# Splitting and turning the maxima of attention 2 one operation at a time, among the next stage's units

## Chip, cores and metric

One core of a Trainium2 chip. The metric is the device time of one execution in microseconds (us). Three runs of the kernel before give 2128.75, 2121.38 and 2128.39 us, so the median is 2128.39.

## What is computed

Two pre-norm blocks over x of shape (4, 512, 256): attention and a mixture of 12 experts, then a second attention and a mixture of 8 experts. The change lies in the second attention, whose keys and values are given:

```python
def _L1_attn_ref(query, kv_k, kv_v, Wq, Wo):     # query = layernorm(x), 4 x 512 rows
    HEADS = 16; HEAD_DIM = 16; SCALE = 1.0 / np.sqrt(HEAD_DIM)
    Q = (query @ Wq.T).reshape(B, QL, HEADS, HEAD_DIM)
    K = kv_k.reshape(KV, HEADS, HEAD_DIM)        # KV = 32 * 128 = 4096 keys
    V = kv_v.reshape(KV, HEADS, HEAD_DIM)
    scores = jnp.einsum('bqhd,khd->bhqk', Q, K) * SCALE
    attn = jax.nn.softmax(scores, axis=-1)
    out = jnp.einsum('bhqk,khd->bqhd', attn, V).reshape(B, QL, HIDDEN)
    return out @ Wo.T
```

## The kernel before, in words

**Stages.** Attention 2 runs in 32 stages (STAGES). A stage H is one pair of heads with the 512 queries of one of the 4 batches: for 4 groups of 4 heads (g), for 4 batches (i), for 2 pairs (h). Within a stage the 4096 keys are taken in 16 steps (NM, the index m; G = 16 H + m counts them over all stages). A step has 4 score products (scores, L1678: 128 keys by 512 queries of one head each, two keys tiles by two heads), 4 exponentials on ScalarE (L1813), and 2 halves of the value products of the step before (values, L1693). Scores are written to three PSUM banks in turn, and the product of a bank waits for the exponential that last read it.

**Maxima.** The softmax subtracts each query's maximum, and it does so inside the score product: two extra rows of the query operand hold the negative maximum, split into a high and a low part, against rows of ones in the keys. So the maxima of stage H + 1 must be known before its first score. They are found while stage H runs, in 32 units (NH). A unit is two products of 128 queries by 512 keys (max_unit, L1096) into one of two pairs of banks, and one reduction over them on VectorE (max_reduce, L1102). TensorE may start a unit when VectorE has done with the unit two before it (the semaphore unit_taken).

**The end of a set of maxima.** After its last unit VectorE makes four small operations, each waiting for the one before:
- max_total (L1112): the maximum over the parts, negated, 128 x 8;
- max_high (L1116): its high part, rounded to the type of the products;
- max_low (L1120): the rest, as a second such number;
- max_turned (L1126): a transpose that puts the parts in rows; it tells rows_ready.

SP then writes the rows to DRAM (store_maxima, L1078), waits for that, reads them into the extra rows of the query operand (load_maxima, two DMAs of L1085) and waits for their landing (L1632). TensorE waits for the same landing (rows_in, L1772) before the first score of the stage.

**The order of the work** is written out by schedule() (L1503). The units of stage H + 1 lie in the steps from G = 16 H - 4 (0 for H = 0) to 16 (H + 1) - 5, two in each step; in TensorE's program one stands after the first two scores of a step and one after the last two. So a set of maxima is complete 4 steps (AHEAD) before its stage begins, and the next step holds the first two units of the set after it. The plan also holds a few other units: late queries (steps 1, 3, 6 and 9 of stages 1 and 3) and, in the last two stages, the output products of earlier batches with residual and normalization (front_results, L1872; steps 11, 12, 14, 15, 16 and so on, counted from the first step of stage 30). The last set of maxima, of stage 31, ends in step 11, where the first front unit stands too, and no maxima follow it. The function unit of VectorE's program (L1824) does what VectorE has to do for one entry of the plan; the loop at L1897 calls it for each step's entries.

**Other queues.** SP also does, in each stage, the fold of the value sums (L1545, L1551), the reciprocals' way through DRAM (L1557, L1560), the packing of outputs (L1569), the loads of keys, values and queries of the next group of heads, and at stage 24 those of the last block's weights. VectorE's reciprocal of the sums (L1870) stands alone between two units, in step 6. GpSimd (POOL) adds and scales the sums (L1650, L1655).

Of the kernel before, what the change touches and what calls it, by code (L numbers as in the profile page):

```python
# [52 lines left out]
def build(nc, a, out):  # L53
    with ExitStack() as ctx:
# [75 lines left out]
        def f32(t):  # L130

            return t.bitcast(F32)
# [860 lines left out]
        with ExitStack() as l1:  # L993
# [110 lines left out]
            def new_maxima(H):  # L1104
                h = H % NP
                return mneg[:, 2 * TB * h:2 * TB * (h + 1)].rearrange("p (r t) -> p r t", r=2)

            def new_parts(H, s):
                return mparts[:, :, s, TB * (H % NP):TB * (H % NP + 1)]
# [4 lines left out]
            def max_high(dve, H):  # L1114
                dve.wait_ge(max_done, H + 1)
                nc.vector.tensor_copy(new_parts(H, 0), new_maxima(H)).then_inc(high_done, 1)  # L1116

            def max_low(dve, H):
                dve.wait_ge(high_done, H + 1)
                nc.vector.tensor_tensor(new_parts(H, 1), new_maxima(H), f32(new_parts(H, 0)), ALU.subtract).then_inc(low_done, 1)  # L1120

            def max_turned(dve, H):
                dve.wait_ge(low_done, H + 1)
                if H:
                    dve.wait_ge(rows_out, 16 * H)
                nc.vector.transpose(mrows[:], f32(mparts[:]).rearrange("p r s n -> p (r s n)")).then_inc(rows_ready, 1)  # L1126
# [376 lines left out]
            def schedule():  # L1503

                plan = [[] for _ in range(STAGES * NM)]
                for H in range(STAGES - 1):
                    begin, end = H * NM - (AHEAD if H else 0), (H + 1) * NM - AHEAD
                    done = 0 if H else EARLY
                    for u in range(done, NH):
                        plan[begin + (u - done) * (end - begin) // (NH - done)].append(("max", H + 1, u))  # L1510
                for c, H in LATE.items():
                    for n, m in enumerate(LATE_AT):
                        plan[H * NM + m].append(("late", c, n))
                for b, kts in enumerate(FRONTS):
                    for n, kt in enumerate(kts):
                        plan[(BATCHES - 1) * NKT + kt].append(("front", b, n))
                return plan

            EARLY = 6
            plan = schedule()  # L1520
# [14 lines left out]
            def unit_bank(n):  # L1535
                return 3 + 2 * (n % 2) if n < LAST_UNIT else WIDE
# [44 lines left out]
            with nc.Block() as block:  # L1581
# [237 lines left out]
                @block.vector  # L1819
                def _(dve):  # L1820
                    ch = Chain(dve, steps[0])
                    units = 0

                    def unit(kind, i, u):  # L1824
                        nonlocal units
                        base = unit_bank(units)
                        dve.wait_ge(unit_mm, units + 1)
                        if kind == "max":
                            max_reduce(NP * u + i % NP, i, base).then_inc(unit_taken, 1)
                            if u == NH - 1:  # L1830
                                wait_unit(dve, units)
                                max_total(i).then_inc(max_done, 1)
                                max_high(dve, i)
                                max_low(dve, i)
                                max_turned(dve, i)
                        elif kind == "late":
                            late_results(i, u, base)
                        elif kind == "front":
                            front_results(i, u, base)
                        elif kind == "turn_out":  # L1840
                            view = ps[:, base, 0:TB * 2 * VR].rearrange("p (t h c) -> p t h c", t=TB, h=2)
                            ch(nc.vector.reciprocal(orec[:], view[:, :, :, DH]))
                            ch.wait()
                            dst = outT[:].rearrange("p (t q h d) -> p t q h d", t=TB, q=2, h=HG)[:, :, (NG - 1) % 2, HG - 2:HG]
                            for t in range(TB):
                                w = nc.vector.tensor_tensor(dst[:, t], view[:, t, :, 0:DH],
                                                            orec[:, t, :].unsqueeze(2).to_broadcast([P, 2, DH]), ALU.mult)
                            w.then_inc(unit_taken, 1)
                        else:
                            rows = slice((NG - 1) % 2 * HG * DH + 2 * DH, (NG - 1) % 2 * HG * DH + HG * DH)  # L1850
                            nc.vector.tensor_copy(aT[rows, NB - 1, (NG - 1) // 2, :], ps[rows, base, :]).then_inc(unit_taken, 1)
                        units += 1

                    def late_results(c, n, bank):
                        m = n % KD
                        if n < KD:
                            nc.vector.tensor_copy(xnT[:, m, :], ps[:, bank, :]).then_inc(unit_taken, 1)
                        else:
                            if c == 3 and m == 0:
                                dve.wait_ge(q_stored, 16 * KD * 3)  # L1860
                            nc.vector.tensor_copy(late_q[:, 0, m], ps[:, bank, :]).then_inc(q_split, 1)
                            dve.wait_ge(q_split, KD * c + m + 1)
                            nc.vector.tensor_tensor(late_q[:, 1, m], ps[:, bank, :], f32(late_q[:, 0, m]), ALU.subtract
                                                    ).then_inc(q_left, 1)
                            dve.wait_ge(q_left, KD * c + m + 1)
                            nc.vector.engine_nop().then_inc(unit_taken, 1)

                    def reciprocals(H):
                        dve.wait_ge(sums_in, 16 * 2 * (H + 1))
                        nc.vector.reciprocal(sums[:], sums[:]).then_inc(rec_done, 1)  # L1870

                    def front_results(b, n, bank):  # L1872
                        rows = lambda t: x[:, TB * b + t, :]
                        if n in (2, 3):
                            nc.vector.tensor_copy(xT1[b][:, n % 2, :], ps[:, bank, :]).then_inc(unit_taken, 1)
                        elif n in (0, 1):
                            t = TB * b + 2 * n
                            nc.vector.tensor_tensor(x[:, t:t + 2, :].rearrange("p t d -> p (t d)"),
                                                    x[:, t:t + 2, :].rearrange("p t d -> p (t d)"), ps[:, bank, :],
                                                    ALU.add).then_inc(unit_taken, 1)  # L1880
                            if n == 1:
                                wait_unit(dve, units)
                                norm_stats(dve, NB + b, rows, main)
                                dve.wait_ge(main.rstd_done, NB + b + 1)
                                if b:
                                    dve.wait_ge(rows1_out, 16 * b)
                                for t in range(TB):
                                    nc.vector.tensor_scalar(xn[:, t, :], rows(t), main.meanvar[:, t, 0:1], main.rstd[:, t:t + 1],
                                                            ALU.subtract, ALU.mult).then_inc(main.norm_done, 1)
                        else:  # L1890
                            take_logits(ch, bank, b, unit_taken)

                    RECIPROCAL = 6

                    for e in first:
                        unit(*e)
                    for G in range(STAGES * NM):  # L1897
                        H, m = divmod(G, NM)
                        if H and m == RECIPROCAL:
                            reciprocals(H - 1)  # L1900
                            if H == STAGES - 1:
                                nc.vector.tensor_tensor(fold, ident[:, 0:2 * VR], ident[:, 2 * VR:4 * VR], ALU.add).then_inc(fold_made, 1)
                        for e in plan[G]:
                            unit(*e)
                    for e in tail:
                        unit(*e)
            clear(step, *main.norm_sems, *l1_used)
# [536 lines left out]
```

## Time and profile before

| what | value |
|---|---|
| median of three runs | 2128.39 us |
| the profiled execution | 2126.7 us |
| its span, first to last instruction | 2125.0 us |
| mean granted TensorE clock | 0.947 |
| PE busy | 1972.1 us, 93% of the span |
| VectorE (DVE) busy | 1559.6 us, 73% |
| ScalarE (ACT) busy | 1346.0 us, 63% |
| GpSimd (POOL) busy | 334.3 us, 16% |

The span is cut into instructions of each engine; PE is TensorE's products, PEld its weight loads, SPq what SP's queue issues. A row of the timeline has the start and the length in us, the engine, the line of the kernel, the operation, the output and inputs, and the number of instructions merged in it; in brackets, the idle time of the engine ahead of it and what ended that. Attention 2's 32 stages lie between about 611 and 1916 us.

### The profile page before, as it was taken

How to read it: one execution, taken by the hardware profiler on the slowest of the kernel's cores; microseconds unless marked ns; L12 is line 12 of the kernel's file. 1: busy time of each engine (PE TensorE's matmuls, PEld its weight loads, DVE VectorE, ACT ScalarE, POOL GpSimd, SP SyncE). 2: the span in 40 equal slices, each digit the busy share in tenths (PEclk: the TensorE clock that was granted, in tenths of full speed). 3: DMA queues.
4: the chain of work that ended last, by engine and by line, in shares of the span. 5: the costliest groups of instructions: out<-in, count | busy, mean ns of one | idle time of the engine just before them, and what ended most of it. 6: DMA issues, size and time to landing. Idle time of an engine off the chain costs nothing. (4 is left out here: it accounts for less than half of the span.)

```text
span 2125.0 us, 40519 instructions
## 1 busy us (share of the span) xinstructions
PE 1972.1 (93%) x15964; PEld 999.5 (47%) x15964; DVE 1559.6 (73%) x2056; ACT 1346.0 (63%) x2652; POOL 334.3 (16%) x333
## 2 busy tenths in 40 slices
PE   6993999997669999999999999999999999998995
PEld 3653889996323333333333333333333333356673
DVE  2537112223689999999999999999999999823454
ACT  1220444441037878888888888888888888764321
POOL 0001334431310100000000000000000000002473
PEclk9995999997569999999999999999999999989997
DMA  4202768865811313103212103222102000001135
GB/s 147 94 21 71 228 221 263 256 212 152 116 19 17 58 46 41 21 11 41 30 33 29 20 14 37 30 37 24 20 17 84 8 9 9 17 26 38 43 102 168
DMA packets 168417, 150.45 MB, mean 71 GB/s; under 512 B 89594, under 2 KB 136678, under 8 KB 167462
## 3 DMA queue, kind: packets, MB, share of 16 engines
q1 hardware_dynamic: 158822, 122.16, 24.8%
q0 software_dynamic: 9408, 25.70, 3.8%
q8 instruction: 128, 2.10, 0.4%
q14 instruction: 59, 0.48, 0.1%
HBM read 108.30 MB, written 32.37 MB: 66 GB/s over the span
## 5 line engine op out<-in xcount | busy, mean ns | idle before, releaser
L1102 DVE TENSOR_REDUCE maxp<-banks 128x2 f32<-128x1024 f32 x1024 | 1224.0, 1220 | 35.0 <-PE banks L1096 34.6
L1813 ACT ACTIVATE pring<-banks 128x512 f32<-128x512 f32 x2048 | 1110.9, 597 | 208.2 <-PE banks L1678 91.2
L1693 PE MATMUL banks<-pring,vcur 128*17 128x256 f32 x8192 | 644.5, 388 | 9.0 <-ACT osb L1807 8.1
L1678 PE MATMUL banks<-qst,kst 50*128 50x512 f32 x2048 | 512.3, 499 | 0.0
L1096 PE MATMUL banks<-kst,qst 50*128 50x512 f32 x2048 | 425.3, 413 | 34.7 <-DVE maxp L1102 18.6
L1678 PEld LDWEIGHTS banks<-qst,kst 50*128 50x128 f32 x2048 | 192.5, 185 | 431.5 <-ACT pring L1813 409.2
L1693 PEld LDWEIGHTS banks<-pring,vcur 128*17 128x17 f32 x8192 | 139.1, 96 | 376.5 <-issue 200.3
L1096 PEld LDWEIGHTS banks<-kst,qst 50*128 50x128 f32 x2048 | 198.6, 191 | 64.4 <-DVE maxp L1102 46.0
L822 ACT ACTIVATE hT<-banks,b 128x128 f32<-128x128 f32 x295 | 107.8, 367 | 188.6 <-PE banks L758 173.8
L960 DVE TENSOR_SCALAR yo<-banks,wblock 128x256 f32<-128x256 f32 x59 | 28.5, 484 | 225.0 <-PE banks L767 225.0
L1650 POOL TENSOR_TENSOR osb<-osb,pairs 64x512 f32<-64x512 f32 x31 | 39.5, 1274 | 727.2 <-DMA pairs<-osb 727.2
L758 PE MATMUL banks<-xgT,w1r 128*128 128x128 f32 x1180 | 144.1, 278 | 1.0 <-issue 1.0
L758 PEld LDWEIGHTS banks<-xgT,w1r 128*128 128x128 f32 x1180 | 138.6, 194 | 2.0 <-issue 1.4
L767 PE MATMUL banks<-w2all,hT 128*128 x590 | 137.8, 381 | 0.0
L767 PEld LDWEIGHTS banks<-w2all,hT 128*128 128x128 f32 x590 | 107.7, 191 | 14.8 <-issue 2.7
L1655 POOL TENSOR_TENSOR osb<-osb,pairs 64x512 f32<-64x512 f32 x31 | 39.6, 1277 | 447.5 <-DMA pairs<-reciprocals 447.5
L711 POOL DMA_INDIRECT expert_rows<-yo,target_i x59 | 61.3, 1039 | 157.8 <-DVE yo L960 152.8
L2128 PE MATMUL banks<-wgu,xgT 128*128 x156 | 52.5, 459 | 0.0
L2365 DVE COPY xgT<-banks 128x256 f32<-128x256 f32 x39 | 16.6, 424 | 36.7 <-PE banks L2141 36.7
L2046 POOL DMA_INDIRECT expert_rows<-yo,target_i x39 | 38.5, 986 | 23.0 <-ACT yo L2228 14.8
L2171 PE MATMUL banks<-wd,hT 88*128 x156 | 40.3, 380 | 1.2 <-DVE hT L2381 1.2
L2040 POOL DMA_INDIRECT xg<-normed_rows,source_i x39 | 38.3, 981 | 11.8 <-issue 9.9
(330 smaller groups left out, 1269.8 us busy)
## 6 DMA issues: line engine op xcount, KB each, us to landing
w1r<-in_L_ffn_w SPq DMA_DIRECT2D x59, 640.0 KB, 4.9
kst<-key_parts SPq DMA_DIRECT2D x18, 512.0 KB
key_parts<-ksp SPq DMA_DIRECT2D x32, 256.0 KB, 2.9
w2all<-in_L_ffn_w SPq DMA_DIRECT2D x12, 640.0 KB, 8.1
qst<-query_parts SPq DMA_DIRECT2D x90, 64.0 KB
kf<-in_kT SPq DMA_DIRECT2D x16, 256.0 KB, 5.6
vcur<-in_v SPq DMA_DIRECT2D x16, 256.0 KB, 9.1
yb<-expert_rows SPq DMA_DIRECT2D x8, 512.0 KB, 7.4
```

The costliest lines, as they stand in the source:

```text
L711: nc.gpsimd.indirect_dma_start(placed, bass.IndirectOffsetOnAxis(ap=target_i[:, b:b + 1], axis=0), yo[b % YO][:], None).then_inc(y_out[b % ...
L758: mm = nc.tensor.matmul(ps[:, HB + n % HR, 0:P], w1r[b % W1R][:, k, i * P:(i + 1) * P], xgT[b % 2][:, k, :], start=(k == 0), stop=(k == KD ...
L767: mm = nc.tensor.matmul(ps[:, YB + b % 2, 0:D], hT[b % 2][:, i, :], w2all[:, bass.ds(e, 1), i, :].rearrange("p o d -> p (o d)"), start=(i ...
L822: nc.scalar.activation(hT[b % 2][:, i, :], ps[:, HB + n % HR, 0:P], ACT.Relu, bias=b1[:, bass.ds(e * NI + i, 1)]).then_inc(h_taken, 1)
L1096: mm = nc.tensor.matmul(ps[:, base + r, :], qst[i][rows, hp, qt * P:(qt + 1) * P], keys[rows, hp, kb * 512:(kb + 1) * 512], start=True, st ...
L1102: return nc.vector.tensor_reduce(maxp[:, :, hp, qt, kb], ps[:, base:base + 2, :], X, ALU.max)
L1655: nc.gpsimd.tensor_tensor(osb[0:2 * VR], osb[0:2 * VR], bc[:], ALU.mult).then_inc(out_done, 1)
L1678: nc.tensor.matmul(ps[:, score_bank(n), :], kst[g % 2][rows, h, kt * P:(kt + 1) * P], qst[i][rows, h, :], start=True, stop=True).then_inc( ...
L1693: mm = nc.tensor.matmul(ps[VR * j:VR * j + VC, 7, cols], vcur[g % 2][:, 2 * m + j // 2, 2 * h + j % 2, :], pring[:, (G % 2) * HG + j, cols ...
L1813: nc.scalar.activation(pring[:, n % (2 * HG), :], ps[:, score_bank(n), :], ACT.Exp, scale=float(DH) ** -0.5).then_inc(exp_done, 1)
L2128: mm = nc.tensor.matmul(ps[:, bank, 0:2 * H1], xgT[b % 2][:, k, :], wgu[:, k, bass.ds(experts[b], 1)].rearrange("p o g h -> p (o g h)"), s ...
L2171: mm = nc.tensor.matmul(ps[:, 5 + u % 2, 0:D], hT[u % 2][0:HC, c, :], wd[:, bass.ds(e, 1), c, :].rearrange("p o d -> p (o d)"), start=(c = ...
```

## The change

VectorE's high part, low part and transpose no longer follow the total at once. They are put off: one of them is made behind each of the next units, or in a step in which the plan has no unit. The total stays where it is. A state of two variables holds the stage that is being turned and the next of the three operations.

```diff
                     ch = Chain(dve, steps[0])
-                    units = 0
+                    units = turning = turn_step = 0
+
+                    def turn_maxima():
+
+                        nonlocal turn_step
+                        if turn_step == 1:
+                            max_high(dve, turning)
+                        elif turn_step == 2:
+                            max_low(dve, turning)
+                        elif turn_step == 3:
+                            max_turned(dve, turning)
+                        turn_step = (turn_step + 1) % 4 if turn_step else 0
 
                     def unit(kind, i, u):
-                        nonlocal units
+                        nonlocal units, turning, turn_step
                         base = unit_bank(units)
                         dve.wait_ge(unit_mm, units + 1)
+                        due = turn_step
                         if kind == "max":
                             max_reduce(NP * u + i % NP, i, base).then_inc(unit_taken, 1)
                             if u == NH - 1:
                                 wait_unit(dve, units)
                                 max_total(i).then_inc(max_done, 1)
-                                max_high(dve, i)
-                                max_low(dve, i)
-                                max_turned(dve, i)
+                                turning, turn_step = i, 1
...
                         units += 1
+                        if due:
+                            turn_maxima()
...
                         for e in plan[G]:
                             unit(*e)
+                        if not plan[G]:
+                            turn_maxima()
```

## Rows read from the trace of the kernel before

**Rows 1.** The page, table of engines and the costliest group.
```profile
PE 1972.1 (93%) x15964; PEld 999.5 (47%) x15964; DVE 1559.6 (73%) x2056; ACT 1346.0 (63%) x2652; POOL 334.3 (16%) x333
...
L1102 DVE TENSOR_REDUCE maxp<-banks 128x2 f32<-128x1024 f32 x1024 | 1224.0, 1220 | 35.0 <-PE banks L1096 34.6
```
**Rows 2.** Windows, stage 10: us; busy PE, PEld, DVE, ACT, POOL; clock; DMA.
```profile
1025.46:1065.05 39.59, 39.30 (x388) 13.92 (x384) 39.10 (x38) 35.14 (x66) 2.55 (x2) 1.00 0.35 39
```
**Rows 3.** Timeline of PE around the end of stage 11's maxima: four score pairs.
```profile
1056.34 0.50 PE L1678 MATMUL banks<-qst,kst 50*128 50x512 f32 x2
...
1057.56 0.49 PE L1678 MATMUL banks<-qst,kst 50*128 50x512 f32 x2
...
1058.95 0.51 PE L1678 MATMUL banks<-qst,kst 50*128 50x512 f32 x2
...
1060.17 0.50 PE L1678 MATMUL banks<-qst,kst 50*128 50x512 f32 x2
```
**Rows 4.** Timeline of PE's weight loads at the same place.
```profile
1057.97 0.19 PEld L1096 LDWEIGHTS banks<-kst,qst 50*128 50x128 f32 x2 [0.23 <-DVE maxp L1102]
```
**Rows 5.** Timeline of VectorE at the same place.
```profile
1054.67 1.23 DVE L1102 TENSOR_REDUCE maxp<-banks 128x2 f32<-128x1024 f32 x1
1055.93 0.22 DVE L1112 TENSOR_REDUCE mneg<-maxp 128x8 f32<-128x64 f32 x1
1056.19 0.17 DVE L1116 CAST mparts<-mneg 128x8 fp32r<-128x8 f32 x1
1056.39 0.17 DVE L1120 TENSOR_TENSOR mparts<-mneg,mparts 128x8 fp32r<-128x8 f32 x1
1056.59 0.21 DVE L1126 STREAM_TRANSPOSE mrows<-mparts 128x32 f32<-128x32 f32 x1
1056.73 5.71 DVE L1102 TENSOR_REDUCE maxp<-banks 128x2 f32<-128x1024 f32 x5
```
**Rows 6.** Timeline of ScalarE behind it.
```profile
1059.49 8.41 ACT L1813 ACTIVATE pring<-banks 128x512 f32<-128x512 f32 x14 [0.32 <-PE banks L1678]
```
**Rows 7.** Waits of 850 to 1810 us: us in total, times, longest.
```profile
PEld banks L1096 <- DVE maxp L1102: 5.4, 24, 0.2
```
**Rows 8.** Timeline of VectorE in step 6: the reciprocal between two reductions.
```profile
1041.16 0.23 DVE L1870 RECIPROCAL sums<-sums 64x16 f32<-64x16 f32 x1
1041.32 3.58 DVE L1102 TENSOR_REDUCE maxp<-banks 128x2 f32<-128x1024 f32 x3
```
**Rows 9.** Timeline of PE: the first scores of stage 11.
```profile
1065.05 0.50 PE L1678 MATMUL banks<-qst,kst 50*128 50x512 f32 x2
```
**Rows 10.** SP's issues of the maxima, stages 10 and 11; issues by line, us to landing.
```profile
1017.24 0.59 SPq L1078 DMA_DIRECT2D maxima<-mrows  x1
1019.71 0.54 SPq L1085 DMA_DIRECT2D qst<-maxima  x2
...
1056.83 0.60 SPq L1078 DMA_DIRECT2D maxima<-mrows  x1
1058.85 0.53 SPq L1085 DMA_DIRECT2D qst<-maxima  x2
...
pairs<-osb SPq DMA_DIRECT2D x29, 128.0 KB, 2.2
...
sums<-osb SPq DMA_DIRECT2D x58, 2.0 KB, 1.7
```
**Rows 11.** Timeline of VectorE and of SP at the end of stage 25's maxima.
```profile
1610.75 0.21 DVE L1126 STREAM_TRANSPOSE mrows<-mparts 128x32 f32<-128x32 f32 x1
...
1614.40 0.59 SPq L1078 DMA_DIRECT2D maxima<-mrows  x1
```
**Rows 12.** Timelines of VectorE and PE: stage 31's maxima and the output products.
```profile
1848.17 0.21 DVE L1126 STREAM_TRANSPOSE mrows<-mparts 128x32 f32<-128x32 f32 x1
...
1855.43 1.38 DVE L1888 TENSOR_SCALAR xn<-x,meanvar,rstd 128x256 f32<-128x256 f32 x4 [1.14 <-POOL rstd L170]
...
1864.58 0.87 PE L1678 MATMUL banks<-qst,kst 50*128 50x512 f32 x4
```

## The prediction
> **What bounds the kernel now.** I read the page's table of engines and its groups first. VectorE is busy for 73% of the span and ScalarE for 63%; VectorE's reductions of maxima (L1102, 1024 of them at 1220 ns) are its largest group by far, and attention 2 is built of them, of ScalarE's exponentials and of TensorE's products. Such shares of the whole span saturate neither [rows 1]. So the question is which of them sets the pace inside a stage. The windows view of one whole stage says: 39.59 us long, PE busy for 39.30, VectorE for 39.10, ScalarE for 35.14, at a granted clock of 1.00 [rows 2]. VectorE's figure deceives. While it keeps pace each reduction is recorded as 1.23 us, but when it is behind, five of them take 5.71 us [rows 5], so one start follows another after (5.71 - 1.22) / 4 = 1.12 us. It can therefore regain 0.10 us per unit; the pace of 1.22 us per half step is set elsewhere, by TensorE and ScalarE handing three score banks to each other.
>
> The timeline of TensorE shows the pace and its one break [rows 3]. The score pairs of L1678 start at 1056.34, 1057.56, 1058.95 and 1060.17: 1.22, 1.39, 1.22. The long interval costs 0.17 us, and it is just where the split and turn of the maxima stand on VectorE [rows 5]. Its cause is named by the weight loads: L1096 at 1057.97 stood idle 0.23 us on VectorE's maxp [rows 4], and ScalarE then had a hole of 0.32 us before its exponentials [rows 6]. TensorE works in order, so one late bank of maxima delays scores, then exponentials. The waits view of 850 to 1810 us has this wait 24 times, 5.4 us in all, 0.2 us at most [rows 7]: once in each of the 24 stages there. The same interval of 1.39 to 1.40 us stands in every stage from 0 to 29 at the same place, 30 times. All 0.17 us of each reach the end, because every later step of TensorE and ScalarE starts that much later and the next stage starts at the same distance.
>
> **The change, part by part.** *Removed*: the run of small operations between the last reduction of a stage's maxima and the first one of the next. Now the total stands at 1055.93 (0.22 us), the high part 0.17, the low part 0.17, the transpose 0.21, and the next reduction starts at 1056.73 [rows 5]. In step it would have started one pitch after 1054.67, at 1055.89. So VectorE falls behind by 0.84 us. How much of that is free? The load that idled was ready at 1057.97 - 0.23 = 1057.74, so a lag of 0.84 - 0.23 = 0.61 us costs nothing.
>
> *Moved*: high, low and transpose each go behind one reduction of the next stage. The total stays. Nothing is added, three small operations and their semaphore updates are as many as before; their waits are on operations that ended over a microsecond earlier, so the 0.03 us gaps between them go. What an operation without such a wait costs in the row is shown by the reciprocal, which already stands alone between two reductions: 0.23 us long, but the next reduction starts 0.16 us after it [rows 8]. By this 0.07 of overlap the lag is: after the total 0.22 + 0.03 - 0.07 = 0.18; then for each unit minus 0.10 regained and plus the small operation: high 0.10, low 0.10, transpose 0.14, so 0.18, 0.18, 0.22. The upper bound takes each at full length with a gap: 0.25, 0.25 - 0.10 + 0.20 = 0.35, 0.45, 0.59. Both stay under 0.61, so the stall goes, wholly by the first and narrowly by the second. I take the first, since the reciprocal is the same case: no stall of TensorE stands at its place. The lower end of the gain is nothing; the upper end is the whole idle time of the load, 30 x 0.23 = 6.9 us.
>
> The Trainium skill speaks against it: "VectorE: DVE Perf Modes", section "The DRAIN you can't avoid", holds that the next operation can't start until the pipe is empty, that semaphores between operations cost nothing extra, and that only the number of operations counts. By it the work moved costs what it did, and a lag would be given back in three parts. The rows differ in a small way, with 0.07 us of overlap where no wait stands.
>
> *What is late next*: the maxima. The transpose's result goes through two DMAs on SP's queue (store L1078, then loads L1085), and TensorE may not start the next stage's scores before they land. Today the transpose ends at 1056.80 [rows 5] and the stage's scores start at 1065.05 [rows 9]: a lead of 8.25 us. Now the third reduction of the next stage starts at 1055.89 + 2.44 + 0.18 = 1058.51, ends some 1.15 later, and the transpose ends at 1059.87, 3.07 us later than now. The scores would start 0.17 earlier, so the lead shrinks to 8.25 - 3.07 - 0.17 = 5.0 us, or 4.6 us by the upper bound of the lag. The need: 0.03 to the store's issue, 2.02 to the loads' issue, half of the pair's 0.54, and a landing like that of the small sums, 1.7 us: 4.0 us. In a slow case the first hop takes 2.47 [rows 10], which makes 4.5. Four or five stages of thirty look like that. The margin is 1.0 us as a rule and 0.1 to 0.5 in those. I cost it at nothing.
>
> *SP and POOL*. SP stands in the wait for the transpose while the moved 3 us pass. Behind it are loads of later queries, for which SP anyway waits for the stage's last scores, and the next fold, which waits for a copy on ScalarE after the first step of the stage. Once SP itself is late: around 1610 it issues the store at 1614.40 although the transpose began at 1610.75 [rows 11]. The new transpose would end there at about 1614.0, so that stage keeps its landing. VectorE's reciprocal at step 6 is some 20 us off. POOL waits for none of the three steps.
>
> *The last turn*, of stage 31 [rows 12], falls among the output products, not among maxima: high after the first residual addition, low after the second with its normalization, the transpose in the next empty step. Now the transpose starts at 1848.17; then it would be at about 1857.0, when the normalization begun at 1855.43 has run its 1.38 us. With 4.5 us of DMAs the rows land by 1861.7, and the scores start at 1864.58: hidden, with nothing gained either, since VectorE was idle between those additions. SP stores the first normed rows behind this landing, so some 5 us later than now; their buffer is written again only within stage 31.
>
> **Sum.** 30 x 0.17 = 5.1 us less than the profiled execution's 2126.7 us: 2121.6. The three runs have the median 2128.39, 1.7 us above the profiled one, so I predict 2123.3, 0.24% less. A measurement of this kernel can tell about 0.5% (10.6 us) from no change, and the three runs shown already spread over 7.4 us.
>
> **The rivals.**
>
> 1. *The stall only moves* (the skill's rule taken strictly). If the small operations cost more than their length and VectorE regains nothing between them, the lag after the fourth is again about 0.8 us and TensorE waits its 0.17 us one or two units later. For it speaks that the upper bound, 0.59, is close to 0.61. Against it speaks the 1.12 us pitch of a late VectorE. Time: as now, 2128.4.
>
> 2. *The rows come too late* (slower). The place is TensorE's wait for the landed maxima before the first score of every stage; each tenth of a microsecond over the lead costs 3 us over 30 stages. It decides from a landing 5.0 us after the transpose on (4.6 by the upper bound). If the first hop took 2.47 everywhere and the last one the 2.2 us of the pairs load [rows 10], the need is 0.03 + 2.47 + 0.27 + 2.2 = 5.0, and against 4.6 that is 0.4 x 30 = 12 us: 2123.3 + 12 = 2135, slower by 0.3%; slower by over 0.5% takes (10.6 + 5.1) / 30 = 0.52 us per stage over the lead. Against it: most first hops take 2.0.
>
> 3. *More comes back than the interval shows*: all 0.23 us of the idle load in each stage, and a run like the lowest one shown, 2121.38: 2121.4 - 6.9 = 2114.5.
>
> That the change does not do what it says is hardly open: the plan has two maxima units in each step after a turn, so all three calls come within one and a half steps.
>
> **How the numbers follow.** Forecast 0.80, rival 1 0.10, rival 2 0.06, rival 3 0.04. The range takes in rivals 1 and 3 and the spread of the runs: 2114.5 to 2130. Faster by over 0.5% needs a result under 2117.8, which only rival 3 or a lucky set of runs gives: 0.06. Slower by over 0.5% is the far half of rival 2: 0.03. Within 0.5%: 0.91.
>
> **What would show it.** Right: score pairs every 1.22 us across the turn; the wait of L1096's loads on maxp gone from the middle stages; stages of 39.41 us instead of 39.59; high, low and transpose each before a reduction that starts at most 0.1 to 0.2 us late; transposes about 5.0 us ahead of the stage. Wrong: a wait of TensorE on the DMA of maxima at a stage's first scores (rival 2), or an interval of over 1.3 us one to three units behind the old place (rival 1).

## The result, and the profile after

Over 12 runs each, the kernel before has a median of 2126.50 us and the changed one 2117.93 us: a ratio of 0.9964, 95% interval 0.9953 to 0.9974. That is 0.36% less where 0.24% was forecast, below the 0.5% that a few runs can tell; the twelve of each, and the same kernel in a later comparison (0.9966, 0.9952 to 0.9981), leave no doubt of the sign. The median lies within the forecast's range, 5.4 us under its value of 2123.3. The profiled execution took 2117.75 us with a span of 2116.0, against 2126.7 and 2125.0.

VectorE's timeline at the end of stage 11's maxima, changed kernel (answers to [rows 5]):

```profile
1045.73 2.45 DVE L1102 TENSOR_REDUCE maxp<-banks 128x2 f32<-128x1024 f32 x2
1048.21 0.22 DVE L1112 TENSOR_REDUCE mneg<-maxp 128x8 f32<-128x64 f32 x1
1048.34 1.22 DVE L1102 TENSOR_REDUCE maxp<-banks 128x2 f32<-128x1024 f32 x1
1049.47 0.16 DVE L1116 CAST mparts<-mneg 128x8 fp32r<-128x8 f32 x1
1049.55 1.22 DVE L1102 TENSOR_REDUCE maxp<-banks 128x2 f32<-128x1024 f32 x1
1050.68 0.15 DVE L1120 TENSOR_TENSOR mparts<-mneg,mparts 128x8 fp32r<-128x8 f32 x1
1050.75 1.22 DVE L1102 TENSOR_REDUCE maxp<-banks 128x2 f32<-128x1024 f32 x1
1051.89 0.20 DVE L1126 STREAM_TRANSPOSE mrows<-mparts 128x32 f32<-128x32 f32 x1
1052.01 2.31 DVE L1102 TENSOR_REDUCE maxp<-banks 128x2 f32<-128x1024 f32 x2
```

The last reduction before the total started at 1045.73 + 1.22 = 1046.95, so in step the next four would start at 1048.17, 1049.39, 1050.61 and 1051.83. They start at 1048.34, 1049.55, 1050.75 and 1052.01: 0.17, 0.16, 0.14 and 0.18 us late, where one of the kernel before was 0.84 late. A reduction with its cast behind it takes 1.21 us of VectorE's time, just under a pitch of 1.22.

TensorE's score pairs over the same stretch, and the first scores of the stage (answers to [rows 3, 9]):

```profile
1048.61 0.50 PE L1678 MATMUL banks<-qst,kst 50*128 50x512 f32 x2
...
1049.83 0.50 PE L1678 MATMUL banks<-qst,kst 50*128 50x512 f32 x2
...
1051.05 0.50 PE L1678 MATMUL banks<-qst,kst 50*128 50x512 f32 x2
...
1052.27 0.50 PE L1678 MATMUL banks<-qst,kst 50*128 50x512 f32 x2
...
1057.15 0.50 PE L1678 MATMUL banks<-qst,kst 50*128 50x512 f32 x2
```

Every interval is 1.22 us. The waits of 842 to 1800 us no longer hold the weight loads' wait on maxp at all; it was 24 times and 5.4 us in [rows 7]. What is left on TensorE in such a stage is its pace and the copy of the value sums.

The windows view cuts both executions at the first scores of stages 0, 1, 30 and 31. The first five rows are the kernel before, the other five the changed one; columns as in [rows 2].

```profile
0.00:611.43 611.43, 506.83 (x2772) 402.03 (x2774) 232.64 (x551) 164.11 (x409) 153.81 (x162) 0.86 0.54 156
611.43:656.89 45.46, 45.02 (x374) 15.84 (x370) 41.43 (x40) 34.34 (x64) 0.00 (x0) 0.85 0.15 9
656.89:1817.14 1160.25, 1151.61 (x11174) 408.75 (x11170) 1140.12 (x1086) 1018.93 (x1886) 79.82 (x63) 1.00 0.18 29
1817.14:1864.58 47.44, 45.99 (x398) 17.74 (x394) 36.85 (x47) 35.08 (x66) 3.58 (x3) 0.93 0.07 18
1864.58:2125.00 260.42, 222.65 (x1264) 155.12 (x1260) 108.54 (x335) 93.53 (x230) 97.14 (x105) 0.93 0.25 77
```

```profile
0.00:607.35 607.35, 503.09 (x2773) 400.90 (x2774) 232.50 (x551) 164.12 (x409) 153.81 (x162) 0.87 0.54 157
607.35:650.86 43.51, 43.07 (x374) 15.27 (x371) 41.34 (x40) 34.35 (x64) 0.00 (x0) 0.89 0.16 10
650.86:1805.93 1155.07, 1146.47 (x11172) 405.95 (x11168) 1137.91 (x1086) 1019.00 (x1886) 79.76 (x63) 1.00 0.18 29
1805.93:1850.62 44.69, 43.24 (x396) 17.27 (x392) 36.67 (x47) 34.59 (x65) 3.58 (x3) 1.00 0.03 8
1850.62:2116.00 265.38, 227.53 (x1264) 158.04 (x1260) 108.58 (x335) 93.88 (x231) 97.11 (x105) 0.90 0.25 78
```

The third row is where the change acts undisturbed: 29 stages at a clock of 1.00, 1160.25 against 1155.07 us, 5.18 less. One more interval lies in stage 0. The other rows differ by -4.1, -2.0 (with that 0.17 in it), -2.8 and +5.0 us, and each goes with its granted clock: 0.86 and 0.87, 0.85 and 0.89, 0.93 and 1.00, 0.93 and 0.90. These are stretches in which TensorE's clock stood at its lower level (1.2 GHz) for a part of the time, and which part differs from one execution to the next. By the traces' clock records it stood there for 226.4 us before and 218.8 us after, never in stages 1 to 29. Stage 30 had 6.8 us of it before and none after, and was 2.75 us longer, so by estimate 0.4 us for each; the 7.6 us less in all would then be worth 3.1 of the 3.8 us that lie outside stages 1 to 29. So of the 9.0 us between the two spans some 5.4 are the change, and most of the rest is the clock that these two executions happened to have.

### The profile page after: what moved, and what is told of

Its sections match the earlier page's. It is cut to its first block and busy times, and to the rows that moved or that the text cites. A ratio compares the mean times of both kernels' runs of the same rounds, so it can differ in the third digit from the quotient of the medians.

```text
span 2116.0 us, 40519 instructions
## 1 busy us (share of the span) xinstructions
PE 1963.4 (93%) x15964; PEld 997.4 (47%) x15964; DVE 1557.0 (74%) x2056; ACT 1345.9 (64%) x2652; POOL 334.3 (16%) x333
## 5 line engine op out<-in xcount | busy, mean ns | idle before, releaser
L1102 DVE TENSOR_REDUCE maxp<-banks 128x2 f32<-128x1024 f32 x1024 | 1236.7, 1221 | 27.6 <-PE banks L1096 27.2
L1096 PE MATMUL banks<-kst,qst 50*128 50x512 f32 x2048 | 420.8, 408 | 34.2 <-DVE maxp L1102 18.9
L2185 PE MATMUL banks<-wd,hT 88*128 x156 | 40.4, 380 | 1.2 <-DVE hT L2395 1.2
```

The lines of the kernel that those rows point to most:

```text
L1096: mm = nc.tensor.matmul(ps[:, base + r, :], qst[i][rows, hp, qt * P:(qt + 1) * P], keys[rows, hp, kb * 512:(kb + 1) * 512], start=True, st ...
L1102: return nc.vector.tensor_reduce(maxp[:, :, hp, qt, kb], ps[:, base:base + 2, :], X, ALU.max)
L2185: mm = nc.tensor.matmul(ps[:, 5 + u % 2, 0:D], hT[u % 2][0:HC, c, :], wd[:, bass.ds(e, 1), c, :].rearrange("p o d -> p (o d)"), start=(c = ...
```

## The experiments

All expectations were written with the result above known, each before its own run. Each comparison has its own runs of the kernel before (medians 2148.58, 2146.03 and 2125.30 us), so ratios are compared and not times. "Lag" is how late a reduction starts against the pitch of 1.22 us.

**All three behind one unit.**

```diff
-                        if turn_step == 1:
+                        if turn_step:
                             max_high(dve, turning)
-                        elif turn_step == 2:
                             max_low(dve, turning)
-                        elif turn_step == 3:
                             max_turned(dve, turning)
-                        turn_step = (turn_step + 1) % 4 if turn_step else 0
+                        turn_step = 0
```

> High, low and transpose together behind the first unit after the total, instead of one behind each of three units. Theory (TensorE waits only for what VectorE's lag has over 0.61 us): the lag behind the first unit is 0.18 - 0.10 + (0.84 - 0.25 - 0.04) = 0.63 us, so the score pairs show at most one interval of 1.22 to 1.25 us in a stage, and the time is that of the changed kernel, 0 to 1 us over it. Rival (what the change took away are the waits between dependent operations, or every operation between two reductions costs its length): the three waits are back, so most of the 0.17 us per stage is back too, interval 1.35 to 1.39, time about 5 us over the changed kernel.

Measured: ratio to the kernel before 0.9971 (0.9948 to 0.9994). VectorE's timeline, then TensorE's, of this kernel at stage 11:

```profile
1048.31 7.33 DVE L1102 TENSOR_REDUCE maxp<-banks 128x2 f32<-128x1024 f32 x6
1055.68 0.22 DVE L1112 TENSOR_REDUCE mneg<-maxp 128x8 f32<-128x64 f32 x1
1055.82 1.22 DVE L1102 TENSOR_REDUCE maxp<-banks 128x2 f32<-128x1024 f32 x1
1056.95 0.16 DVE L1116 CAST mparts<-mneg 128x8 fp32r<-128x8 f32 x1
1057.14 0.17 DVE L1120 TENSOR_TENSOR mparts<-mneg,mparts 128x8 fp32r<-128x8 f32 x1
1057.35 0.21 DVE L1126 STREAM_TRANSPOSE mrows<-mparts 128x32 f32<-128x32 f32 x1
1057.48 1.18 DVE L1102 TENSOR_REDUCE maxp<-banks 128x2 f32<-128x1024 f32 x1
```

```profile
1057.30 0.50 PE L1678 MATMUL banks<-qst,kst 50*128 50x512 f32 x2
...
1058.53 0.51 PE L1678 MATMUL banks<-qst,kst 50*128 50x512 f32 x2
```

The last reduction before the total started at 1048.31 + 7.33 - 1.22 = 1054.42. The reduction of 1057.48 is therefore 0.62 us late (in step it would be at 1056.86), and the interval is 1.23: this lag is still free, as the 0.61 us of the prediction said to within what can be read. The waits between dependent operations are back and cost nothing, so they were not the gain. Most stages take 39.41 us as in the changed kernel; two took 0.7 us more, which is told below, and so stages 1 to 29 are 1.4 us over the changed kernel's where 0 to 1 was expected.

**The same work twice, in a lump and spread.** High and low are each made once more, into the same place; the second half of the diff is alike for low.

```diff
             def max_high(dve, H):
                 dve.wait_ge(max_done, H + 1)
+                if H:
+                    nc.vector.tensor_copy(new_parts(H, 0), new_maxima(H)).then_inc(again, 1)
+                    dve.wait_ge(again, 2 * H - 1)
                 nc.vector.tensor_copy(new_parts(H, 0), new_maxima(H)).then_inc(high_done, 1)
```

In the kernel before (lump):

> The kernel before, with the high and the low part each made twice in stages 1 to 31, each waiting for the one before: the lump grows by 2 x 0.20 us. Theory (stall = lag over 0.61): the lag is 0.84 + 0.40 = 1.24 us, the interval grows from 1.39 to about 1.79, 30 x 0.40 = 12 us over the kernel before. Rival (TensorE's stall is a fixed price of having a break there): interval 1.39, time of the kernel before.

In the changed kernel (spread):

> The changed kernel with the same two additions as in the twice-made lump, but spread with the rest: 0.30, 0.30 and 0.14 us behind three units, each less 0.10 regained. Theory: lags 0.18, 0.38, 0.58, 0.62, so no stall or one of 0.01 us; time of the changed kernel within 1 us, 17 us under the twice-made lump although VectorE's work is the same. Rival (VectorE's work in attention 2 is the bound, wherever it stands): 30 x 0.40 = 12 us over the changed kernel.

Measured against the kernel before, in the same comparison: lump 1.0049 (1.0031 to 1.0068), spread 0.9966 (0.9951 to 0.9981). The lump's score pairs:

```profile
1064.26 0.49 PE L1685 MATMUL banks<-qst,kst 50*128 50x512 f32 x2
1066.06 0.49 PE L1685 MATMUL banks<-qst,kst 50*128 50x512 f32 x2
```

An interval of 1.80 us, 1.79 expected, and stages of 39.99 us instead of 39.59. Stages 1 to 29 took 1172.57 us, 12.3 more than in the kernel before, with 12 expected for 30. Its VectorE rows at this place:

```profile
1058.94 3.66 DVE L1103 TENSOR_REDUCE maxp<-banks 128x2 f32<-128x1024 f32 x3
...
1063.84 2.31 DVE L1103 TENSOR_REDUCE maxp<-banks 128x2 f32<-128x1024 f32 x2
```

In step the reduction of 1063.84 would start at 1058.94 + 3.66 = 1062.60, so the lag is 1.24 us. VectorE's timeline of the spread one:

```profile
1045.89 4.89 DVE L1103 TENSOR_REDUCE maxp<-banks 128x2 f32<-128x1024 f32 x4
...
1050.95 1.22 DVE L1103 TENSOR_REDUCE maxp<-banks 128x2 f32<-128x1024 f32 x1
...
1052.36 1.22 DVE L1103 TENSOR_REDUCE maxp<-banks 128x2 f32<-128x1024 f32 x1
...
1053.77 1.22 DVE L1103 TENSOR_REDUCE maxp<-banks 128x2 f32<-128x1024 f32 x1
...
1055.03 2.31 DVE L1103 TENSOR_REDUCE maxp<-banks 128x2 f32<-128x1024 f32 x2
```

Against a last start in step at 1045.89 + 4.89 - 1.22 = 1049.56 the lags are 0.17, 0.36, 0.55 and 0.59, expected 0.18, 0.38, 0.58 and 0.62; the score pairs stay 1.22 to 1.23 us apart. VectorE's work is the same in both kernels, and they differ by 0.83% (1.0049 against 0.9966), some 18 us. So VectorE's amount of work is not the bound of attention 2. What counts is how much of it stands in one place. Which of TensorE and ScalarE sets the pace of 1.22 us no run here tells.

**Later by two units and by one.** The deadline behind the maxima. The diff for two units; for one, the steps are 2, 3, 4 and the modulus 5.

```diff
-                        if turn_step == 1:
+                        if turn_step == 3:
                             max_high(dve, turning)
-                        elif turn_step == 2:
+                        elif turn_step == 4:
                             max_low(dve, turning)
-                        elif turn_step == 3:
+                        elif turn_step == 5:
                             max_turned(dve, turning)
-                        turn_step = (turn_step + 1) % 4 if turn_step else 0
+                        turn_step = (turn_step + 1) % 6 if turn_step else 0
...
-                                turning, turn_step = i, 1
+                                turning, turn_step = i, 1 if i < STAGES - 1 else 3
```

> The three operations wait two units more (behind the third, fourth and fifth unit after the total; stage 31's turn as in the changed kernel). Theory (the rows are the next deadline): the transpose ends 2.44 us later, 5.07 - 2.44 = 2.63 us ahead of the stage, the landing needs 3.65 to 3.8 us, so TensorE waits some 1.1 us at the first scores of 30 stages: 30 to 33 us over the changed kernel, about 26 us over the kernel before. Rival (the rows' landing is not what holds a stage's first scores): no wait there, time of the changed kernel.

> The three operations wait one unit more than in the changed kernel (stage 31's as there). Theory: the lead of the transpose's end over the stage's first scores is 5.07 - 1.22 = 3.85 us, the landing needs 3.63 to 3.85 us after it, with slow cases of 4.2: mostly no wait, up to 0.1 us in some stages and 0.4 in one or two; 0 to 2 us over the changed kernel. The deadline lies here, between one and two units later. Rival (other work on SP sets when the maxima land, not the transpose): no change at all against the changed kernel, and the same landing time.

Measured against the kernel before: two later 1.0111 (1.0083 to 1.0139), one later 0.9984 (0.9969 to 0.9999). Two units later: VectorE's, SP's and TensorE's timelines at stage 11, and the waits of 868 to 1830 us:

```profile
1071.13 0.20 DVE L1126 STREAM_TRANSPOSE mrows<-mparts 128x32 f32<-128x32 f32 x1
...
1071.36 0.61 SPq L1078 DMA_DIRECT2D maxima<-mrows  x1
1073.39 0.53 SPq L1085 DMA_DIRECT2D qst<-maxima  x2
...
1075.04 0.50 PE L1678 MATMUL banks<-qst,kst 50*128 50x512 f32 x2 [0.87 <-DMA qst<-maxima]
...
PE banks L1678 <- DMA qst<-maxima: 22.1, 24, 1.0
```

The first scores of stage 11 wait for the landing, and so do those of each of the 24 stages in the window, 22.1 us in all, and a stage takes 40.4 us instead of 39.4: about 1.0 us per stage where 1.1 was expected, 28.9 us over stages 1 to 29. The rows' landing is the next bound, and it begins 3.7 us after the transpose's end (1075.04 - 1071.33). With one unit less of delay the lead is 3.93 us; the last interval before a stage is longer than 1.22 us in only three of 30 cases (1.41, 1.36 and 1.37 us, ahead of stages 3, 21 and 25), and stages 1 to 29 took 1155.42 us, 0.35 over the changed kernel's first profile and level with its second. Its median is nevertheless 0.16% under that of the kernel before where 0.25% was expected; the interval includes both.

**Without the last turn, and the last turn alone.** In the first, stage 31's three operations follow its total at once and the others are put off; the second is the reverse (condition i < STAGES - 1).

```diff
-                                turning, turn_step = i, 1
+                                if i == STAGES - 1:
+                                    max_high(dve, i)
+                                    max_low(dve, i)
+                                    max_turned(dve, i)
+                                else:
+                                    turning, turn_step = i, 1
```

> The change for stages 1 to 30 alone; stage 31's high, low and transpose follow its total at once, as before. Theory (all of the gain is 30 stages of 0.17 to 0.18 us, the rest of the difference measured is where TensorE's clock stands at half): time of the changed kernel, 5 to 6 us under the kernel before; stages of 39.41 us. Rival (the last turn, put off among the output products, gives some 2 to 3 us of its own): 2 to 3 us over the changed kernel.

> The change for stage 31's maxima alone, all others turned at once as before. Theory: time of the kernel before within 1 us, intervals of 1.39 us in every stage. Rival: 2 to 3 us under the kernel before.

Measured against the kernel before: all but the last 0.9972 (0.9956 to 0.9989), the last alone 1.0006 (0.9987 to 1.0025). Windows of stages 1 to 29, all but the last and then the last alone:

```profile
650.20:1805.20 1155.00, 1146.37 (x11172) 405.26 (x11168) 1137.86 (x1086) 1018.95 (x1886) 79.77 (x63) 1.00 0.19 29
...
651.14:1811.62 1160.48, 1151.45 (x11174) 408.33 (x11170) 1140.38 (x1086) 1019.35 (x1886) 79.72 (x63) 1.00 0.19 29
```

The two differ by 5.48 us. Of these 0.48 are one interval of 1.88 us in stage 4 of the last alone, of the kind told at the end; the other 5.0 are 29 times 0.17. The change acts in these stages, and the last turn gives nothing that can be told from no change. Stage 30 took 44.67 us in both, so the 47.44 of the profile before was a matter of the clock, not of the code.

**Two and one; the changed kernel once more.** High and low behind the first unit, the transpose behind the second:

```diff
                         if turn_step == 1:
                             max_high(dve, turning)
-                        elif turn_step == 2:
                             max_low(dve, turning)
-                        elif turn_step == 3:
+                        elif turn_step == 2:
                             max_turned(dve, turning)
-                        turn_step = (turn_step + 1) % 4 if turn_step else 0
+                        turn_step = (turn_step + 1) % 3 if turn_step else 0
```

> High and low behind the first unit after the total, the transpose behind the second. Theory: lags 0.18, 0.18 - 0.10 + 0.28 = 0.36, 0.36 - 0.10 + 0.13 = 0.39 us, all under 0.61: stages of 39.41 us and no wait on the banks of maxima, time of the changed kernel within 1 us, while the transpose ends 6.3 us ahead of the stage instead of 5.07. Rival (each operation must have a reduction to itself): an interval over 1.3 us, 3 to 5 us over the changed kernel.

> The changed kernel once more, for the size of the gain. Theory (only the 30 intervals): 5.4 us, ratio 0.9975, and any excess over it in a single profile lies where TensorE's granted clock is 0.50 and turns up in either direction. Rival (something beyond the 30 intervals gives 2 to 4 us in every run): ratio 0.9955 to 0.9965 again.

Measured: 0.9961 (0.9949 to 0.9973) and 0.9966 (0.9952 to 0.9981). Two and one is level with the changed kernel, with stages of 39.40 us, while the transpose ends 6.07 us ahead of the stage instead of 5.07. (6.3 was expected: two operations behind one unit leave VectorE later than one does.) The repeat gave 0.9966, near the rival's figures, though its interval includes the theory's 0.9975; that of the first comparison, up to 0.9974, just leaves it out. What lies beyond the 30 intervals is taken up under the sum.

## Why the prediction was right, point by point

- *The break in the pace and its price.* Right. Before, stages take 39.59 us, now 39.41; 1160.25 against 1155.07 us for 29 of them, 5.4 us with stage 0's. Forecast was 5.1, from 0.17 us read off two starts.
- *The free lag of 0.61 us.* Right in kind and 0.05 too small: lags of 0.59 and 0.62 cost nothing that the stages' lengths show, 0.84 cost 0.17 and 1.24 cost 0.58, and the last two leave 0.67 and 0.66 free. The prediction took the load's idle time of 0.23 us for what the lag had over, where the interval had grown by 0.17 only. The sum used the 0.17, so nothing hung on it but the price of rival 3.
- *The price of an operation without a wait.* Right: lags of 0.17, 0.16, 0.14 and 0.18 against 0.18, 0.18, 0.18 and 0.22. The first of the two ways of costing was the true one, and the reciprocal was the right row to read it from. The cast of 0.16 us moved the next reduction by 0.08 (1049.47 to 1049.55). The prediction read the Trainium skill more strictly than it is written: "VectorE: DVE Perf Modes", section "The DRAIN you can't avoid", adds that a next operation that is not held starts earlier. With that the row agrees. What the section says of semaphores, that they cost nothing extra, these rows do not bear out: in a chain in which each operation waits for the one before, as in [rows 5], one start follows the other after 0.20 us.
- *The lead of the rows.* Right: 5.0 us forecast, 1057.15 - 1052.09 = 5.06 found; the need was 3.6 to 3.8 us instead of 4.0, so the margin is 1.3 us as a rule. The slow first hop was seen in one stage, with 0.87 us left.
- *Rival 1*, the stall only moves: fell with the lump behind one unit. *Rival 2*, the rows come too late: its mechanism is real, but it decides two units further on. *Rival 3*, all of the load's idle time comes back: fell, for a stage gave back 0.18 us and not 0.23. Its time of 2114.5 is nevertheless nearer to the median found, 2117.93, than the forecast's 2123.3 is. Of the 5.4 us to the forecast, 1.9 are the starting point (three runs had a median of 2128.39, twelve have 2126.50) and 3.5 the larger difference.
- *SP and POOL.* SP cost nothing, as said: in the changed kernel's stage 25 the store is issued 0.03 us after the transpose, like the others. That POOL waits for none of the three steps is true of its program; that VectorE may be held by POOL was not thought of, and the forecast has no term for it. It cost 0.05 us in one profile of the changed kernel and 0.4 in the other (last section).
- *The last turn.* Nothing gained, as said. Its margin was 0.98 us and not some 3: the transpose ended at 1845.93 and stage 31 began at 1850.62. The forecast took that stage's start from an execution whose stage 30 was 2.8 us longer by the clock alone.
- *The sum.* The median came out 8.6 us lower, the forecast was 5.1. The kernels that have the 30 intervals removed and nothing else of note (the changed one twice, without the last turn, spread twice, two and one) gave 0.9961 to 0.9972, that is 6 to 8 us. The trace shows 5.2 to 5.4 of them. The other 1 to 3 us lie outside stages 1 to 29, where the profiles scatter more than that: stage 0 alone took from 42.5 to 48.1 us over these executions. A part is luck with the clock. Fitted over the runs of each comparison, 0.001 of a run's mean granted clock goes with 1.6 to 2.1 us; at equal clock the difference to the kernel before is 5.2 us without the last turn, 5.3 spread twice, 5.9 in one lump, 6.6 for the changed kernel and 7.0 for two and one, each with a standard error of 0.5 to 0.7. So the first two have nothing beyond the intervals, and in the last two some 1 to 2 us stay open. Nor do the runs show that a faster attention 2 raises the clock: beside the kernel before, the mean of it is 0.0006 higher in the changed kernel and 0.0014 spread twice, but only 0.0001 in one lump and without the last turn. That term, the effect outside the stages, was costed at nothing.

## What to carry to other kernels

An engine that is busy all the time in a profile may still have slack, and the slack has two sizes: what it regains per unit when it is behind (here 0.10 us) and how late it may be before its consumer's buffer is missing (here between 0.62 and 0.67 us). Housekeeping put into a pipeline costs nothing while each piece keeps the lag below the second; the same work in one piece costs its excess each time. Before it is put off, look up the deadline of what it makes: here three units were free, four nearly so, and five cost a microsecond in every stage. When a small gain is to be sized, compare undisturbed windows rather than whole spans.

## What was not expected

VectorE's small operations on SBUF are at times held by GpSimd. VectorE and then GpSimd, the kernel with all three behind one unit, end of stage 3's maxima; then the same of the changed kernel at stage 25's:

```profile
734.88 0.89 DVE L1116 CAST mparts<-mneg 128x8 fp32r<-128x8 f32 x1
...
734.47 1.28 POOL L1655 TENSOR_TENSOR osb<-osb,pairs 64x512 f32<-64x512 f32 x1 [20.15 <-DMA pairs<-reciprocals]
```

```profile
1602.37 0.68 DVE L1120 TENSOR_TENSOR mparts<-mneg,mparts 128x8 fp32r<-128x8 f32 x1
...
1601.75 1.27 POOL L1655 TENSOR_TENSOR osb<-osb,pairs 64x512 f32<-64x512 f32 x1 [25.36 <-DMA pairs<-reciprocals]
```

The cast, 0.16 us elsewhere, took 0.89 and ended at 735.77, as GpSimd's multiplication ended at 735.75; the subtraction took 0.68 instead of 0.15 and ended at 1603.05, GpSimd at 1603.02. Reductions out of PSUM beside such a multiplication were not held. In the lump this made one interval of 1.91 us (stage 2). In the changed kernel's first profile it made one of 1.27; in the second a cast of 0.96 us at stage 2 made one of 1.55, beyond the free lag too, and stage 24 had one of 1.30. So spreading does not protect from it. The eleven profiles have nine such operations, of 0.42 to 0.96 us, all in stages 2, 4 and 24 and all ending within 0.04 us of the multiplication; the profile of the kernel before has two casts of 0.21 instead of 0.17, with intervals of 1.44 instead of 1.39 to 1.40, which the prediction took for the same. These are stages in which SP is late with the reciprocals and GpSimd's work slides to the end of the maxima. The Trainium skill has the mechanism in "SBUF — State Buffer", section "Terms": VectorE and GpSimd share a pair of ports, held for a whole instruction, and the other one blocks. The rows agree: each held operation ends with GpSimd's. Another late SP made the lump's second long stage: the waits of that kernel have one wait of 0.6 us of the scores on the maxima's DMA, at stage 25.
